# A gated attention and expert block on one core: four copies of each value product, and products without a use in idle places of TensorE

## The reference, cut to what matters

```python
# attention, per sequence and head (q from the normalised x, k = v = ctx)
cs = cumsum(log_sigmoid(fg)); log_D = where(lower triangle, cs[s] - cs[t], -inf) + ig[t]
D_mat = exp(log_D - rowmax(log_D))
C = (q @ k.T) / sqrt(32) * D_mat
h = C / (max(abs(C.sum(-1)), exp(-rowmax)) + 1e-6) @ v
x = x + tanh(g_xattn) * layernorm(h) * ln_scale
# experts, on layernorm(x)
hidden = square(relu(x @ w1[e].T)); moe_out = sum over 2 chosen e of (hidden @ w2[e].T) * w[e]
shared = square(relu(x @ cfc.T)) @ cproj.T
x = x + tanh(g_ffn) * (moe_out + shared)
```

## Time and profile before

| | |
|---|---|
| median of 3 runs | 307.25 us (306.86 to 309.63) |
| profiled execution | 307.44 us, of which span 305.4 us |
| mean granted clock of TensorE | 0.790 |
| PE busy | 225.1 us, 1660 matmul records |
| DVE busy | 195.0 us |
| ACT busy | 142.2 us |
| POOL busy | 141.3 us |
| DMA | 46.94 MB, 154 GB/s |

### The profile page before, as it was taken

The page is one execution under the profiler, slowest core; times in us unless marked ns, Lnnn a source line. Parts: engine busy times, 40 slices in busy tenths (PEclk is TensorE's granted clock), DMA queues, the critical chain, the costliest instruction groups (busy, mean ns, idle before and its releaser), DMA issues.

```text
span 305.4 us, 5288 instructions
## 1 busy us (share of the span) xinstructions
PE 225.1 (74%) x1660; PEld 182.4 (60%) x1660; DVE 195.0 (64%) x454; ACT 142.2 (47%) x264; POOL 141.3 (46%) x183
## 2 busy tenths in 40 slices
PE   0378029998989979999983908958899997987200
PEld 0234018987878869888882507535688886865100
DVE  7893882466856754984409886794578733947442
ACT  2665434456454475325511386524367745754100
POOL 4896143544169509530670737572000034664772
PEclk9989755999775587555575885788999999999955
DMA  7999981355723212400150216493989998999863
GB/s 171 372 168 154 345 328 36 90 159 169 212 83 120 66 41 68 106 0 0 38 155 17 87 52 156 105 374 87 144 116 231 209 208 207 187 194 348 260 182 103
DMA packets 74395, 46.94 MB, mean 154 GB/s; under 512 B 52737, under 2 KB 68481, under 8 KB 74241
## 3 DMA queue, kind: packets, MB, share of 16 engines
q1 hardware_dynamic: 64896, 30.09, 42.4%
q0 software_dynamic: 3216, 10.49, 11.0%
q10 hardware_dynamic: 6256, 6.03, 7.7%
HBM read 20.12 MB, written 17.83 MB: 124 GB/s over the span
## 4 chain that ended last, share of the span: by engine, by line
PE 56%; DVE 12%; DMA 11%; issue 6%; POOL 4%; SPq 4%; ACT 3%; another core or an unknown queue 2%; POOLq 1%; DVEq 0%; ACTq 0%
PE bank L700 10%; PE bank L853 8%; PE bank L866 7%; DMA qT<-xs 5%; PE bank L719 3%; PE bank L675 3%; PE bank L673 3%; PE bank L671 3%; DMA x_all<-x 3%; PE bank L739 2%; PE bank L746 2%; POOL kT L614 2%; PE bank L685 2%; PE bank L637 2%
## 5 line engine op out<-in xcount | busy, mean ns | idle before, releaser
L614 POOL DMA_INDIRECT kT<-ys,slot_y x32 | 33.2, 1039 | 58.2 <-DMA ys<-heads 44.6
L700 PE MATMUL bank<-vaug,heads 128*128 128x33 f32 x256 | 43.6, 324 | 3.5 <-DVE h_sum L1296 3.5
L700 PEld LDWEIGHTS bank<-vaug,heads 128*128 128x128 f32 x256 | 42.6, 251 | 4.1 <-DVE heads L1260 4.0
L1260 DVE SCALAR_TENSOR_TENSOR heads<-bank,heads 128x512 f32<-128x512 f32 x32 | 22.0, 688 | 32.2 <-ACT heads L980 24.8
L980 ACT ACTIVATE heads<-bank 128x512 f32<-128x512 f32 x32 | 19.1, 596 | 34.3 <-PE bank L675 34.0
L853 PE MATMUL bank<-qT,w_hi 128*128 128x256 bf16 x184 | 31.5, 273 | 4.3 <-DMA qT<-xs 3.5
L525 POOL TENSOR_TENSOR w_lo<-w_stage,w_hi 128x1024 bf16<-128x1024 f32 x9 | 19.4, 2151 | 16.9 <-ACT w_hi L985 16.9
L866 PE MATMUL bank<-w_hi,h_n 128*128 x92 | 25.1, 273 | 2.2 <-issue 2.2
L1543 DVE TENSOR_TENSOR vaug<-vaug 128x512 f32<-128x512 f32 x23 | 15.9, 691 | 15.4 <-ACT vaug L1128 11.6
L866 PE MATMUL bank<-w_lo,h_n 128*128 x92 | 25.1, 272 | 0.5 <-issue 0.5
L853 PE MATMUL bank<-qT,w_lo 128*128 128x256 bf16 x92 | 25.1, 273 | 0.1
(11 more groups left out here) (248 smaller groups left out, 578.4 us busy)
## 6 DMA issues: line engine op xcount, KB each, us to landing
ys<-heads ACTq DMA_DIRECT2D x23, 256.0 KB
w_stage<-experts SPq DMA_DIRECT2D x9, 512.0 KB, 5.0
q_pad<-parts SPq DMA_DIRECT2D x36, 128.0 KB, 2.6
x_all<-x SPq DMA_DIRECT2D x4, 512.0 KB, 7.1
w_hi<-ctxT SPq DMA_DIRECT2D x4, 512.0 KB, 7.7
vaug<-ctx SPq DMA_DIRECT2D x16, 128.0 KB, 3.9
out<-x_all SPq DMA_DIRECT2D x16, 128.0 KB
parts<-kT SPq DMA_DIRECT2D x3, 512.0 KB, 5.4
```

The lines of the kernel that those rows point to most:

```text
L614: g.indirect_dma_start(out=y_tok[:, t % GB, k, :], out_offset=None, in_=ys[0:DONE[t] * UNIT], in_offset=bass.IndirectOffsetOnAxis(ap=slot_ ...
L700: last = mm(bank[4 + c // 2][:, at:at + DV], p_sb[:, j % PS, c * P:(c + 1) * P], vaug[:, b, c, j, :], start=True, stop=True)
L1260: v.scalar_tensor_tensor(p_sb[:, j % PS, :], bank[2 + j % 2][:], SCALE, d_sb[:, j % 2, :], ALU.mult, ALU.mult).then_inc(p_ok, 1)
```

## The change

It has three parts, and adds no transfer and no work to another engine.

1. Each value product streams its 33 columns four times: the moving operand is `vaug[:, b, c, j:j + 1, :]` broadcast four times, and the output 132 columns. The surplus copies land in columns that the next heads of the group write, or behind them; each chunk now has 256 columns of a bank in place of 132 (UNIT = 256), and DVE's two additions read the first 132 of each.
2. A function `keep_busy(to, n)` issues n products of 512 columns whose result nobody reads: 10 into bank 1 as soon as `a_ok` is up and 8 more behind the transposes of the rows (L798), both ahead of the attention.
3. The same function behind the attention: 12 ahead of `places(1)`, 12 ahead of the transposes of batch 3 (once the relu of batch 0 are done), 8 ahead of `up(2)` (once those of batch 1 are done).

```diff
+            def keep_busy(to, n):
+                for _ in range(n):
+                    mm(to[:], ident_b[:], mask[:].rearrange("p c s -> p (c s)"), start=True, stop=True)
...
-                    at = (c % 2) * GV + (j % 4) * DV
-                    last = mm(bank[4 + c // 2][:, at:at + DV], p_sb[:, j % PS, c * P:(c + 1) * P],
-                              vaug[:, b, c, j, :], start=True, stop=True)
+                    at = (c % 2) * UNIT + (j % 4) * DV
+                    last = mm(bank[4 + c // 2][:, at:at + 4 * DV].rearrange("p (r d) -> p r d", r=4), p_sb[:, j % PS, c * P:(c + 1) * P],
+                              vaug[:, b, c, j:j + 1, :].to_broadcast([P, 4, DV]), start=True, stop=True)
...
+            pe.wait_ge(const_ok, 3)
+            pe.wait_ge(a_ok, 1)
+            keep_busy(bank[1], 10)
             pe.wait_ge(rows_ok, 1)
             pe.wait_ge(state_row_ok, 1)
...
             last.then_inc(rows_psum, 1)
+            keep_busy(bank[1], 8)
...
             head_values(B - 1, NH - 1)
+            pe.wait_ge(exp_ok, B * NH)
+            keep_busy(bank[0], 12)
             places(1)
...
             places(2)
+            pe.wait_ge(relu_ok, KC)
+            keep_busy(bank[0], 12)
             transpose_x(3, (2, 3))
...
             places(3)
+            pe.wait_ge(relu_ok, 2 * KC)
+            keep_busy(bank[4], 8)
             up(2)
...
-                v.tensor_tensor(h4[:, 0:2], bank[4][:, 0:2 * GV].rearrange("p (c g) -> p c g", c=2), carried[:, 0:2], ALU.add)
-                v.tensor_tensor(h4[:, 2:4], bank[5][:, 0:2 * GV].rearrange("p (c g) -> p c g", c=2),
+                v.tensor_tensor(h4[:, 0:2], bank[4][:].rearrange("p (c g) -> p c g", c=2)[:, :, 0:GV], carried[:, 0:2], ALU.add)
+                v.tensor_tensor(h4[:, 2:4], bank[5][:].rearrange("p (c g) -> p c g", c=2)[:, :, 0:GV],
                                 carried[:, 2:4], ALU.add).then_inc(comb_ok, 1)
```

## The result

| | before | changed |
|---|---|---|
| median of the runs | 307.06 us (306.09 to 309.63, 4 runs) | 295.88 us (293.34 to 303.86, 4 runs) |
| profiled execution, its span | 307.44, 305.4 | 293.34, 291.6 |
| granted clock over the span | 0.790 | 0.878 |

The ratio is 0.960, with a 95% interval of 0.950 to 0.969: faster by 4%. The profile of the changed kernel, in the order of the earlier trace rows. Lines have moved: the value products are L704, the short f32 group L723, L750 the router, L743 the transposes, L849 the down products, L653 the added products, L1299 and L1338 are L1285 and L1324 of before.

The account below looks back on a forecast made before the run. TensorE at its lower clock level was taken to set the pace in batches 2 and 3. Savings of 13.3 + 3.9 + 2.0 - 1.5 = 17.7 us gave 289.7 against 307.44, or 289.5 against the median; range 281 to 301.

Parts of the forecast that it names:

- M1 to M2: From the mean of batch 1's attention statistics to batch 2's: 0.8 us saved before the value products, 1.5 after.
- M2 to M3: From the mean of batch 2's attention statistics to batch 3's: 3.1 us saved before the value products, 3.2 after.
- M3 to E: From the mean of batch 3's attention statistics to the last L1285: 13.7 us before, 3.9 saved, a middle value.
- rival 1: Value products, batches 1 to 3: level doesn't follow the columns; 314.3 us, chance 0.07, or 308.3 with the start helped, 0.07.
- The price of the wide group: Value products of each head: 0.12 us more at the upper level, 0.26 at the lower; groups at 0.98 us per head.
- POOL's chain sets batches 2 and 3: Batches 2 and 3: first value products wait for POOL, then DVE; 13.45 us from the mean in batch 2, 14.0 in 3.
- Batch 0: First attention batch: upper level from 45.7 to 54.3 us saves 4.3, less 0.7 for six wider heads: 3.5 us.
- Behind the attention: Added products after the attention and the steps they precede: between -1.9 and +3.0 us, taken as 2.0 saved.
- rival 4: All waits fold: L1285 follows directly behind L729, and 3 us are saved behind the attention; 284 us, chance 0.18.
- rival 2: End of the attention: the scatters hold DVE, so the 13.7 us there stay; 293.6 us, chance 0.2.
- Rival 3: TensorE's new waits of some 4 us per batch drop the level, each drop costing 2 to 3; 297.5 us, chance 0.15.
- The expert stage keeps its length.: Expert stage: no gain, since its clock is up already and transfers and 1.31 us groups set it.

Follow-up runs that it names:

- Values alone: The changed kernel with the value products streamed four times but none of the 50 added products: 286.25 us, ratio 0.961 to the kernel before.
- two streams: The changed kernel with value products streamed twice (66 columns) in place of four times (132): 290.12 us, ratio 0.984 to the kernel before.
- Group 3: Against the changed kernel: POOL's keys and residual ahead of the third low part, 0.989; that with gaps behind the attention filled, 0.964; 17 products ahead of the decay product, 0.972.
- groups 1 and 2: Experiments on two chips, on parts of the change and on disputed places (second dozen, gaps, 66 columns); kernel before 297.75 and 295.09 us.
- groups 3 and 4: Experiments on two more chips, on POOL's order, 17 products ahead of the decay product, and the latter with gaps filled; kernel before 309.21 and 310.06 us.
- before again: The kernel before, unchanged, run and profiled once more on the chip of the second group of experiments: 294.95 us.

## Why the prediction was right, and where it was off

The sign, the range and the main mechanism held; the forecast of 289.5 was 6.4 us too low, outside my own band of 286 to 292. Term by term, in us:

| term | predicted | profile |
|---|---|---|
| batches 0 and 1, until M1 | 4.7 | 2.25 |
| M1 to M2 | 2.3 | 3.0 |
| M2 to M3 | 6.3 | 6.2 |
| M3 to E | 3.9 | 5.5 |
| behind the attention | 2.0 | -5.3 |
| drops of level | -1.5 | within the above |
| experts and the rest | 0 | 2.2 |

- *Wider value products bring the level up* (rival 1 against it): shown. Values alone 0.961, added products alone 1.002, two streams 0.984, with the clock from M2 to M3 at 0.93, 0.66 and 0.88. This is the cause of the gain. Narrow heads alone don't explain the low level, though, and I read the earlier trace rows too simply: the slices from 53 to 76 us, inside the attention, stand at 9, and the same narrow heads ran at 0.81 and 0.88 in the first two batches.
- *The price of the wide group*, 0.98 us a head: the chain of waits has L704 at 0.90 to 0.96 for a head at the upper level, where the narrow one has 0.81 to 0.87 (the earlier trace rows show one of 0.87). Right, a little cheaper. DVE's two additions take 0.42 us each before and after, so nothing was right for them.
- *POOL's chain sets batches 2 and 3.* In batch 2, 13.45 us from the mean to the value products were predicted, 13.52 came. Group 3 showed the chain to be on the path (the value products moved with it), and also that it isn't all: shorten it, and DVE is held by POOL's next operation. I had left that coupling out. In batch 3 the sum fits (6.3 and 6.2) in part by luck: the value products came at 14.9, not 14.0, and the rest of the step took 11.2, not 12.0.
- *Batch 0: 3.5 us.* The term was mis-sized: the prediction let the level stay up once the first heads find it. It did start high, but was at the lower level from 46.6 to 53.5 us in this execution, with TensorE busy without a gap. Of nine profiled executions with 8 products ahead of the decay product, each with 1.2 or 1.9 us of idle time behind them, it fell in seven (D to M1 37.1 to 39.0) and held in two (35.1 and 35.5); with 17 it held in both (35.5), with none it was low until 53 to 55 in all three (40.0 to 40.9). So the full step is about 5 us, and the change as made gets 1 to 2 of it most times. That the gap is the reason is likely, not shown: two of two executions with it filled stand against two of nine without, and one of those two had the whole 1.9 us.
- *Behind the attention: +2.0.* The step that failed. I had the second dozen at "nothing or 1.7"; by the profile it delayed the transposes by 3.1, since the wait for relu came out only 1.9 us ahead of the rows (164.8 against 166.7) where the earlier trace rows had 3.2, and it ran at the lower level. Over all profiles the transposes start 0.9 to 3.3 us behind DVE's rows in the six that have the dozen there, and under 0.1 behind them in the eight that don't. In E to T it is 25.3 to 26.3 us against 21.9 in groups 1 and 2 (23.2 in the first profile of the kernel before), but 24.6 and 25.6 against 23.8 and 24.3 in groups 3 and 4, where the rows came later too. The rest of the -5.3 has no cause shown and did not come again: on the second chip E to U was 54.0 in the changed kernel and 55.2 in the kernel before.
- *M3 to E.* It followed L729 (now L733), as in rival 4; rival 2 (the scatters) is out. But the wait it was to save was of one execution: before again has 9.2 for this step, and 7.7 to 9.2 is what the wide kernels have, so the lasting gain is about 1 us. Some 4 of the table's 5.5 us are luck in the execution that stood for the kernel before.
- *Rival 3.* The time came near its 297.5, but not in its way: the waits of 2 to 3 us came in batches 2 and 3, and the clock stayed at 0.92 to 0.93 from M1 to E.
- *"The expert stage keeps its length."* It is 63.1 to 82.8 us long in the profiles with the same instructions, and this sets how well the rest can be seen: on the second chip the attention gave 12.4 us (D to E 111.2 against 98.8) and the experts took 6.3 back in those two profiles, with TensorE waiting 7.7 us for units in one and not in the other:

```profile
PE bank L861 <- DMA qT<-xs: 7.7, 4, 2.8
```

What stays open: why that stage varies, why the narrow heads ran at the upper level in part of the attention, and what ACT waits for in batch 3 on the chips of groups 3 and 4 (M2 to M3 27.2 to 28.4 against 26.1 in six other profiles with wide products).

## What to carry to other kernels

Where TensorE is busy without a gap and still at its lower level, look at how many columns each product streams: repeating a narrow product's moving operand into unused columns of the same bank cost 0.02 us a product here (0.96 against 0.87 us for four), and the step from M2 to M3 went from 30.1 to 33.4 us down to 26.1 to 28.4. Products added elsewhere, to keep the engine busy, gave nothing by themselves here. Where one adds them all the same, these runs speak for time that is idle in the new schedule, and against a place behind a wait that may end late. And when the bound goes over to another engine, its neighbours' coupling is part of the price.

## What the runs showed of the hardware

- The granted clock from M2 to M3: 0.57, 0.59 and 0.66 with value products of 33 columns (three profiles), 0.88 with 66 (one), 0.88 to 0.94 with 132 (ten), at busy shares of TensorE of 0.96 to 0.99, 0.84, and 0.81 to 0.86. The kernels that stream more columns are the less busy ones, at the higher level. From M1 to M2 the narrow kernels differ more, 0.64, 0.74 and 0.82, against 0.87 with 66 columns and 0.87 to 0.98 with 132.
- In batch 0 the level held both times with the gap ahead of the decay product filled, and in two of nine executions without. The Trainium skill, page "TensorE: Matmul & The Clock Gate", section "Why this matters for your kernels", asks for no idle gaps between bursts of matmuls, but means longer ones than the 1.9 us here. These runs neither confirm nor refute it for this gap; in the narrow batches the level was low without a gap.
- A VectorE operation on two operands in SBUF stood still while GpSimd ran a tensor operation: 2.16 us in place of 0.21 (L1316), ending with it, in both kernels with the two low parts together. It isn't of that order alone: in the changed kernel L1288, two operands too, takes 1.25 us in place of 0.36 and ends at 93.92, where GpSimd's L514 ends at 93.76. The Trainium skill, page "GPSIMD Engine Reference", section "Specifications", says that the two share their SBUF interfaces; the trace agrees.
- The kernel before differs by 5% between the four groups and their chips (295.09 to 310.06 us); the ratio of the changed kernel to it was 0.960 and 0.961 on the two chips where it was measured.
